# One two-tensor comparison of 1024 elements instead of four comparisons of 256 with a scalar, in a one-hot table look-up

## What is computed

```python
e = jnp.stack([tbl_0[ids[:, 0]], tbl_1[ids[:, 1]], ..., tbl_25[ids[:, 25]]], axis=1)   # 2048 x 26 x 128
all_vecs = jnp.concatenate([dense_proj[:, None, :], e], axis=1)                         # 27 vectors
interactions = jnp.einsum('bnd,bmd->bnm', all_vecs, all_vecs)
z = jnp.concatenate([dense_proj, interactions[:, rows, cols]], axis=1)                  # rows < cols: 351 pairs
h = jnp.concatenate([z, r_dense_proj], axis=1)
h = jnp.maximum(h @ W_top1 + b_top1, 0.0)     # 512
h = jnp.maximum(h @ W_top2 + b_top2, 0.0)     # 256
y = h @ W_top3                                # 2048 x 1
```

## Time and profile before

| | |
|---|---|
| median of three runs | 452.38 us (450.32 to 454.48) |
| the profiled execution | 455.76 us |
| its span, first to last instruction | 453.8 us |
| TensorE busy | 377.8 us, 6224 products |
| VectorE busy | 254.9 us, 767 instructions |
| GpSimd busy | 231.0 us, 244 instructions |
| ScalarE busy | 146.3 us, 265 instructions |
| mean granted clock of TensorE | 0.947 of its full speed |

### The profile page before, as it was taken

How to read it: one execution, slowest core, us unless ns; L and a number is a source line. 1 busy time by engine, 2 the same in 40 slices (tenths; PEclk the granted TensorE clock), 3 DMA queues, 4 the chain that set the end, 5 groups by cost and what they waited for, 6 DMA issues and landing times.

```text
span 453.8 us, 14936 instructions
## 1 busy us (share of the span) xinstructions
PE 377.8 (83%) x6224; PEld 341.5 (75%) x6224; DVE 254.9 (56%) x767; ACT 146.3 (32%) x265; POOL 231.0 (51%) x244
## 2 busy tenths in 40 slices
PE   0769993968989799887998789887999788998877
PEld 0758893967887688876897689776998687886645
DVE  5997798663534865456555766456654765321110
ACT  2355130413313342333323342332413351335212
POOL 4365656465465454556555555555565535556000
PEclk9998996878996999999899999999998998999969
DMA  7999925151431314132341517151343411111000
GB/s 182 230 225 231 241 60 105 34 103 46 80 77 49 83 40 104 40 83 68 60 84 45 99 41 85 60 102 49 66 90 53 86 29 40 40 40 48 4 1 0
DMA packets 25441, 36.37 MB, mean 80 GB/s; under 512 B 5378, under 2 KB 19594, under 8 KB 25417
## 3 DMA queue, kind: packets, MB, share of 16 engines
q1 hardware_dynamic: 17577, 20.27, 24.6%
q0 software_dynamic: 7680, 15.74, 12.9%
q10 hardware_dynamic: 160, 0.01, 0.0%
HBM read 35.99 MB, written 0.01 MB: 79 GB/s over the span
## 4 chain that ended last, share of the span: by engine, by line
PE 69%; DVE 12%; issue 11%; DMA 3%; POOL 2%; ACT 1%; SPq 0%; DVEq 0%; ACTq 0%
PE hid L421 11%; DVE onehot L607 9%; PE look_ps L379 8%; PE look_ps L377 8%; PE gram L449 8%; PE look_odd L379 6%; PE hid L428 6%; PE look_odd L377 6%; PE vec_act L332 5%; POOL vecs L315 2%; DMA vecs<-tbl,ids_sb 2%; PE hid L377 2%; PE hid L379 2%; PE look_odd L374 2%; PE small L390 2%
## 5 line engine op out<-in xcount | busy, mean ns | idle before, releaser
L315 POOL DMA_INDIRECT vecs<-tbl,ids_sb x240 | 230.8, 962 | 187.0 <-issue 121.0
L607 DVE TENSOR_SCALAR onehot<-step_ids,row_no 125x256 fp32r<-125x256 int32 x704 | 210.6, 361 | 141.4 <-PE look_ps L379 49.0
L377 PE MATMUL look_ps<-onehot,look_hi 125*128 125x256 f32 x312 | 85.1, 305 | 7.8 <-DVE onehot L607 3.9
L580 ACT COPY vecs_T<-vec_act 128x512 f32<-128x512 f32 x64 | 37.6, 597 | 151.7 <-remote 67.3
L379 PE MATMUL look_ps<-onehot,look_lo 125*128 125x256 f32 x312 | 80.6, 291 | 1.6 <-issue 1.6
L449 PE MATMUL gram<-vecs_T 128*27 128x26 f32 x4096 | 50.3, 197 | 22.6 <-issue 22.5
L377 PEld LDWEIGHTS look_ps<-onehot,look_hi 125*128 125x128 f32 x312 | 62.2, 199 | 8.6 <-issue 8.1
L449 PEld LDWEIGHTS gram<-vecs_T 128*27 128x27 f32 x4096 | 43.9, 108 | 31.4 <-issue 28.1
L377 PE MATMUL look_odd<-onehot,look_hi 125*128 125x256 f32 x240 | 63.8, 300 | 1.9 <-issue 1.8
L379 PEld LDWEIGHTS look_ps<-onehot,look_lo 125*128 125x128 f32 x312 | 62.2, 199 | 3.4 <-issue 3.2
L379 PE MATMUL look_odd<-onehot,look_lo 125*128 125x256 f32 x240 | 60.1, 284 | 2.8 <-issue 2.7
(11 more groups left out here) (89 smaller groups left out, 325.7 us busy)
## 6 DMA issues: line engine op xcount, KB each, us to landing
step_ids<-look_ids SPq DMA_DIRECT2D x7, 768.0 KB
table_raw<-tbl SPq DMA_DIRECT2D x11, 448.0 KB
step_ids<-look_ids SPq DMA_DIRECT2D x7, 640.0 KB
vecs<-tbl,ids_sb POOLq DMA_INDIRECT x240
step_ids<-look_ids SPq DMA_DIRECT2D x11, 128.0 KB, 10.8
vecs<-dense SPq DMA_DIRECT2D x16, 64.0 KB
table_raw<-tbl SPq DMA_DIRECT2D x11, 52.0 KB
w_sb<-w SPq DMA_DIRECT2D x1, 512.0 KB
```

What stands on the lines that cost most here:

```text
L315: nc.gpsimd.indirect_dma_start(out=vecs[j][:, 1 + k, :], out_offset=None, in_=tables[k], in_offset=bass.IndirectOffsetOnAxis(ap=ids_sb[:, ...
L377: nc.tensor.matmul(bank, look_hi[:, f, ch, :], onehot[:, SLOT[g], c, :], start=ch == 0, stop=False)
L580: return engine_copy(vecs_T[j][:, :, 1 + lo:1 + hi], bank[:, 0:hi - lo, :].rearrange("d v b -> d b v"))
L607: last = nc.vector.tensor_scalar(onehot[:, SLOT[g], c, :], step_ids[a][0:LOOK_K, f - TABLES_OF[a][0], :], row_no[0:LOOK_K, ch:ch + 1], Non ...
```

## The change

`make_unit` issues one VectorE instruction for a unit in place of four. It compares two tensors: the 256 ids, read four times over (stride 0 in the chunk), and four columns of `row_no`, each read 256 times over (stride 0 in the example). The result goes to the whole slot, 125 x 1024. The waits around it and the count that follows it stay.

```diff
                     if positive(unit_count(pair, g) - SLOT_BACK[g]):
                         dve.wait_ge(onehot_used, unit_count(pair, g) - SLOT_BACK[g])
-                    for c in range(UNIT_CH):
-                        ch = half * UNIT_CH + c
-                        last = nc.vector.tensor_scalar(
-                            onehot[:, SLOT[g], c, :], step_ids[a][0:LOOK_K, f - TABLES_OF[a][0], :],
-                            row_no[0:LOOK_K, ch:ch + 1], None, ALU.is_equal)
-                    last.then_inc(onehot_made, 1)
+                    rows = row_no[0:LOOK_K, half * UNIT_CH:(half + 1) * UNIT_CH]
+                    ids_of = step_ids[a][0:LOOK_K, f - TABLES_OF[a][0], :]
+                    nc.vector.tensor_tensor(
+                        onehot[:, SLOT[g], :, :], ids_of.unsqueeze(1).broadcast_to([LOOK_K, UNIT_CH, PAIR]),
+                        rows.unsqueeze(2).broadcast_to([LOOK_K, UNIT_CH, PAIR]), ALU.is_equal).then_inc(onehot_made, 1)
```

## The result

The changed kernel takes 469.41 us, the median of four runs (464.24 to 473.68); the kernel before takes 453.43 us beside it. The ratio is 1.034, with a 95% interval of 1.028 to 1.040. It is slower by 16 us; the forecast was 452.7 us, no change. The profiled execution of the changed kernel took 473.68 us, with a span of 471.7. It is a slow one, with a clock of 0.917 where the other three runs have 464.24 to 469.73 us and 0.920 to 0.926, so its waits are on the large side.

What follows compares the result with a forecast made beforehand. TensorE, 83% busy, was taken to depend on one-hot speed for at most 11.0 us. Bursts 0.0 (+0.5), start 0 (+0.7), rest 0, taken as +0.3 us, gave 452.7 us; range 449.6 to 458.

Steps and rivals of the forecast that it cites:

- The price of a unit: At L607, one 1024-element two-tensor instruction was to take 1.22 us, where four instructions alone are busy 1.14 us.
- Rival 1: At L607, repeated or mixed-type reads make a unit 1.63 us long; time 467 us, chance 7%.
- The bursts: Five VectorE stretches, from the first unit after slots are freed to L587: 28.19 against 28.29 us, cost 0.0 to +0.5.
- the start: Until 36 us VectorE works without pause: +0.7 us of work, taken as hidden, so 0, or +0.7 if not.
- The sign that five turns would still be waited for at L390: TensorE at L390 would still wait five times for VectorE's L596, 7 to 8 us in total.
- Rival 2: VectorE's units wait for GpSimd's gathers, 0.35 us a unit; time 463 us, chance 5%.
- the guess beside it: The skill's port rule, by which VectorE's scalar instructions and GpSimd contend, would explain bursts of 5.32 us instead of 4.78.
- A rule weighed against rows: Step setting the skill's shared-port rule against L617 beside gathers (1206 to 1227 ns): by the rows, units wait for nothing.
- "Rest 0": Everything outside the bursts and the start, including other L390 turns and VectorE's total one-hot time, was to cost 0 us.
- Rival 4: Buffers and gathers, started when TensorE frees rows, fall otherwise: a few us either way, no sign favoured; chance 4%.
- The ranges of the unit's price: Bounds for a unit at L607: 1.08 us from below, 1.63 us from above, around the 1.22 taken.

Runs made afterwards that it cites:

- e14: Kernel before, with eight of fifteen gathers a tile from tile 2 on and later ids loaded to 16 partitions only: 389.9 us.
- e15: Changed kernel, with eight of fifteen gathers a tile from tile 2 on and later ids loaded to 16 partitions only: 389.7 us.
- e7: Changed kernel, with the ids of pairs 1 to 7 loaded to 16 partitions in place of 128: 413.6 us, 1.006 of the kernel before.
- e8: Kernel before, with the ids of pairs 1 to 7 loaded to 16 partitions in place of 128: 402.1 us, 0.970 of the unmodified one.

## Why the prediction was wrong

- **The price of a unit: right.** 1225 ns against 1.22 us taken from L617, with repeated reads and int32 beside float32. Rival 1 (1.63 us) did not come.
- **The bursts and the start: right as a sum of VectorE.** Units that do not wait for a slot advance by 1.26 to 1.35 us, against 1.32. A burst of six takes 7.88 us against 7.75, the one of four 5.10 against 5.11. From the first L617 to the eighth (L616 now, 8.49 to 35.09) are 26.60 us against 26.46; that the eighth starts where it did (35.07) is since the first starts 0.8 us earlier. Where rows are early (e14, e15), the two kernels are equal to 0.2 us. The sign that five turns would still be waited for at L390 did not come (one is).
- **Rival 2, units wait for gathers: did not come.** No unit is longer than 1270 ns. But the guess beside it, that a gather makes some of today's units long, is borne out by the trace of the kernel before: of the 704 instructions at L607, 79 take over 0.40 us, all beside a gather, and 77 of these start 0.5 to 0.7 us after the gather does (0.42 us at 12.26, 0.55 at 72.74, where the median is 0.35).
- **The step that failed is "A rule weighed against rows".** It asked only whether VectorE would wait for GpSimd, and read the earlier trace rows for the length of L617. The same rows held the answer to the other question. The gather at 64.78 is 1.75 us long. It starts under an L617 that began at 64.51 and ran to 65.74, so 0.96 us were left, and 0.96 + 0.82 = 1.78. Its neighbours take 0.96 and 1.01. Two more gathers of that trace start well under an L617, at 9.81 (1.51 us) and 21.22 (1.09), and fit as well. The text used these rows as proof that nothing waits. The Trainium skill ("SBUF — State Buffer", section "Who interferes with whom") says that of the two the second to issue stands still; the traces agree for a gather behind a unit (1.91 us for 0.94), and differ for a two-tensor unit behind a gather, of which none of 124 is held (1.24 us at most). The same section of the Trainium skill also tells of a probe in which a tensor_tensor did not stall DMA work of GpSimd, and gives a reason that it marks as inferred; these gathers are stalled, and the measurement decides.
- **"Rest 0" in the sum fell with it.** Between 100 and 400 us of the trace of the changed kernel 63 of 162 gathers take over 1.05 us, in that of the kernel before 4 of 175 do, by little (1.08 at most). From 962 to 1116 ns over 240 gathers are 37 us of GpSimd. In place of the 0, the runs show 16 us in all, and 11.5 of them without the collision with the ids load (e7, e8). Before, GpSimd was 51% busy, and the text asked nothing of it. But its rows are wanted at a given point: in the changed kernel's loop the rows of odd tiles come late, behind fifteen gathers. The waits for rows were 7.6 us in two places already, and the chain that ended last went through GpSimd and its DMA: a lead that the prediction didn't follow, since it looked for waits behind VectorE alone.
- **What the shift brings on top was not in the sum at all:** two second halves of gathers meet the ids load (10.6 us from issue to rows), and TensorE falls to its lower clock level in the wait and for 4 us after it. With small loads the loss is 11.5 us in place of 15.1.
- **The chances.** 14% stood on slower. Rival 4, shifts of buffers and gathers, came nearest, with 2% on slower and "a few us", and it did not name what lengthens a gather. The ranges of the unit's price were no measure of what the change could do to another engine.

What stays open: how the 11.5 us of e7 against e8 divide. TensorE's waits for rows differ by 4.3 us there (15.6 and 11.3), and the mean granted clock is 0.967 against 0.979, which is (0.033 x 411.5) - (0.021 x 400.6) = 5.2 us of full-speed work not done. These two give 9.5, but they overlap, and no run parts them. Open too is what the growing idle time "for issue" at L449 is, in the traces of the slower chips.

## What to carry to other kernels

Before a VectorE instruction is given a second tensor in SBUF, look at what GpSimd does at that time, and read both engines' rows for both directions: who is longer when they overlap. Three overlong gathers beside the only long two-tensor instruction of the kernel before were enough to know it. And an engine at 51% may be full where it matters: ask when its result is wanted, not how busy it is.

Fewer and larger VectorE instructions are not a gain in themselves here. Four scalar instructions of 256 elements leave the gathers at 962 ns, one of 1024 draws them out to 1075, and two tensors do so at either size (1045 and 1116). Why the short scalar ones don't is not shown.

## What the runs showed of the hardware

- A gather (indirect DMA by GpSimd) that starts while a VectorE instruction with two SBUF inputs runs waits until that ends and then needs 0.82 us (1.91 us where 1.10 were left, 1.68 where 0.85 were left; 127 of 129 gathers to 0.03 us). One that has started 0.16 us earlier isn't touched (0.94), nor are those that start 0.01 to 0.03 us earlier. With one input in PSUM a unit of the same length holds none but one by 0.14 us (955 ns on the mean, against 1100).
- A tensor_scalar over 1024 elements from int32 to float32 in SBUF takes 0.75 us, a tensor_tensor over as many 1.225. The short one holds gathers too (1.55 us), and is held itself (0.88). Of 256 elements it does not hold them (962 ns on the mean), and is held by one that started 0.5 to 0.7 us before it (up to 0.55 us for 0.35); a two-tensor instruction isn't.
- Gathers issued beside a load of 768 KB had their rows 10.6 us after the last issue, where 2.1 to 2.7 is usual; halving the bytes of these loads gave 2.2% of the whole kernel, cutting the same bytes into eleven loads gave nothing.
- After a wait of TensorE with the granted clock at 0.50, it was still 0.50 over the next 4 us of products without a pause (0.21 us from one to the next, in place of 0.12).
